# A padded DRAM copy of all edge attributes, written during the layer-0 passes of a graph network kernel

## The reference, cut to what matters

```python
# layer 0: two graph attention passes (forward over dst, backward over src), no edge attributes
x = x + gat_fwd_bwd(layernorm(x), edge_index)
x = x + experts(layernorm(x))
# layer 1
q, k, v = (z @ Wq + bq), (z @ Wk + bk), (z @ Wv + bv)     # z = layernorm(x)
e   = edge_attr @ We
k_j = k[src] + e
v_j = v[src] + e
alpha = segment_softmax(sum(q[dst] * k_j) / sqrt(32), dst)  # 8 heads of 32
out   = segment_sum(v_j * alpha, dst) + z @ Ws + bs
x = x + out
x = x + slice_attention(layernorm(x))
```

## Time and profile before

| | |
|---|---|
| Median of 3 runs | 5683.37 us (5675.45 to 5690.65) |
| Span of the profiled execution, first to last instruction | 5673.3 us |
| DVE busy | 3824.3 us (67%) |
| POOL busy | 3388.4 us (60%) |
| PE busy | 2860.0 us (50%) |
| ACT busy | 1441.9 us (25%) |
| POOL's DMA queue, share of the 16 engines' span | 28.6%, 483.60 MB |
| SP's DMA queue, share of the 16 engines' span | 24.9%, 476.59 MB |

### The profile page before, as it was taken

One profiled execution on the slowest core, in us unless ns is written; L12 is line 12 of the kernel. 1 busy time (PEld: TensorE's weight loads), 2 busy tenths in 40 slices (PEclk: granted clock), 3 DMA queues, 4 the chain that ended last, 5 costly groups with the idle time before them and its releaser, 6 DMA issues. The chain is left out here.

```text
span 5673.3 us, 49658 instructions
## 1 busy us (share of the span) xinstructions
PE 2860.0 (50%) x13052; PEld 2232.1 (39%) x13052; DVE 3824.3 (67%) x6117; ACT 1441.9 (25%) x2526; POOL 3388.4 (60%) x3382
## 2 busy tenths in 40 slices
PE   7513200000000000015899986888888888884777
PEld 5412200000000000014677633777776777673456
DVE  7357778786454545546543464989899998995763
ACT  1113333332233333311222211222222222221320
POOL 0267777777777777753440276777777777773200
PEclk9655555555555555556799998999999999896888
DMA  3133344432363333323232355999999999993114
GB/s 101 36 84 108 107 130 148 130 104 83 103 220 110 109 110 109 110 87 124 93 124 68 107 191 191 317 319 323 319 319 321 319 323 318 323 318 113 67 47 148
DMA packets 290231, 961.79 MB, mean 170 GB/s; under 512 B 79248, under 2 KB 119831, under 8 KB 248468
## 3 DMA queue, kind: packets, MB, share of 16 engines
q0 software_dynamic: 171296, 483.60, 28.6%
q1 hardware_dynamic: 118788, 476.59, 24.9%
HBM read 626.03 MB, written 345.69 MB: 171 GB/s over the span
## 5 line engine op out<-in xcount | busy, mean ns | idle before, releaser
L1249 PE MATMUL e_psE<-e_we,e_eaT 128*128 128x256 f32 x3136 | 903.5, 415 | 279.3 <-DVE e_wv L1148 179.3
L1111 POOL DMA_INDIRECT e_kv<-kv,rec x784 | 875.7, 1117 | 266.3 <-issue 253.7
L779 POOL DMA_INDIRECT g_g<-t,rec x784 | 777.1, 991 | 254.0 <-issue 253.7
L779 POOL DMA_INDIRECT g_g<-t,dst_of x784 | 743.6, 949 | 259.3 <-issue 257.2
L1249 PEld LDWEIGHTS e_psE<-e_we,e_eaT 128*128 128x128 f32 x3136 | 649.4, 210 | 400.7 <-ACT e_eaT L1192 299.4
L1407 PE MATMUL j_psM<-ident,tail 128*128 128x128 f32 x32 | 7.2, 416 | 1149.0 <-PEq L53 1149.0
L1250 PE MATMUL e_psE<-e_kv,ident 128*128 128x256 f32 x1568 | 509.8, 409 | 0.0
L816 DVE TENSOR_TENSOR_SCAN g_wv<-g_fx,g_wv 128x2176 f32<-128x2176 f32 x98 | 459.0, 4684 | 0.2 <-issue 0.2
L1407 PEld LDWEIGHTS j_psM<-ident,tail 128*128 128x128 f32 x32 | 6.8, 322 | 1149.8 <-issue 1149.8
L1118 POOL DMA_INDIRECT e_q<-q,q_of x392 | 370.9, 946 | 119.7 <-issue 119.7
L956 ACT ACTIVATE g_st<-g_wv 128x2048 f32<-128x2048 f32 x98 | 375.9, 3836 | 0.0
(11 more groups left out here) (519 smaller groups left out, 6620.8 us busy)
## 6 DMA issues: line engine op xcount, KB each, us to landing
state<-e_st SPq DMA_DIRECT2D x98, 1088.0 KB, 6.2
e_ea<-in_edge_attr SPq DMA_DIRECT2D x98, 896.0 KB, 9.8
state_f<-g_st SPq DMA_DIRECT2D x49, 1088.0 KB, 4.4
state_b<-g_st SPq DMA_DIRECT2D x49, 1088.0 KB, 4.3
m_work<-xs SPq DMA_DIRECT2D x119, 128.0 KB, 2.3
ys<-m_work SPq DMA_DIRECT2D x119, 128.0 KB, 1.7
xs<-g_ta SPq DMA_DIRECT2D x28, 512.0 KB
g_g<-t,rec POOLq DMA_INDIRECT x784
```

The lines of the kernel that those rows point to most:

```text
L779: pool.indirect_dma_start(g[:, u, j, :], None, tab, bass.IndirectOffsetOnAxis(ap=at_, axis=0)).then_inc(gat[u], 16)
L1111: pool.indirect_dma_start(kv[:, u, b, :], None, c.kv, bass.IndirectOffsetOnAxis(ap=c.rec[:, t, 1:2], axis=0)).then_inc(gkv[u][b // 4], 16)
L1249: nc.tensor.matmul(half, eaT[:, m, j, k, :], we[:, k, :], start=(k == 0), stop=False)
```

## The change

All 128 partitions' attributes are copied during the layer-0 passes, in blocks 0 to 97, one or two partitions in each block (128 partitions over 98 blocks), to a new DRAM buffer `c.ea_p`. Its rows, one for each partition, are one attribute row (1 KB) longer than they need be: neighbouring partitions lie 785 KB apart. The edge pass loads each block with one DMA for all 128 partitions from that buffer, whether the edges were sorted or not; `order_attributes` writes there if its flag is set. SP reads no flag in the edge pass and has no branch. `c.ea_sorted` and `c.ea_tail` are gone.

```diff
-            def copy_attributes(a):
+            def copy_attributes(p):
+                ea, lo = A["edge_attr_256"], p * T
+                real = min(T, E - lo)
+                spread = lambda at, n: c.ea_p[p:p + 1, at * D:(at + n) * D].rearrange("o (a n) -> (o a) n", a=16)
                 over_engines = lambda rows: rows.rearrange("(a n) w -> a (n w)", a=16)
-                ea, lo = A["edge_attr_256"], (112 + a) * T
-                real = min(T, E - lo)
-                sp.dma_start(over_engines(c.ea_tail[a * T:a * T + real, :]), over_engines(ea[lo:lo + real, :])).then_inc(other, 16)
+                sp.dma_start(spread(0, real), over_engines(ea[lo:lo + real, :])).then_inc(other, 16)
                 if real == T:
                     return 1
-                sp.dma_start(over_engines(c.ea_tail[a * T + real:(a + 1) * T, :]), over_engines(ea[0:T - real, :])).then_inc(other, 16)
+                sp.dma_start(spread(real, T - real), over_engines(ea[0:T - real, :])).then_inc(other, 16)
                 return 2
...
-                if 0 <= blk - FIRST < 16:
-                    others += copy_attributes(blk - FIRST)
+                for p in range(blk * P // NB, (blk + 1) * P // NB):
+                    others += copy_attributes(p)
...
-                        sp.dma_start(c.ea_sorted.rearrange("(p t) w -> p (t w)", p=P)[:, bass.ds((i * U + u) * (B * D), B * D)],
+                        sp.dma_start(c.ea_p[:, bass.ds((i * U + u) * (B * D), B * D)],
                                      rows[:, u, :, :]).then_inc(so[u], 16)
...
-            unsorted = c.flag_on(sp)
 
             def load_attributes(b, u):
 
-
-                at_ = bass.ds(b * (B * D), B * D)
-                rows = lambda a: a.rearrange("(p t) w -> p (t w)", t=T)[:, at_]
-                with sp.If(unsorted > 0):
-                    sp.dma_start(ea[0:112, u, :, :], rows(c.ea_sorted[0:112 * T, :])).then_inc(eg[u], 16)
-                    sp.dma_start(ea[112:P, u, :, :], rows(c.ea_sorted[112 * T:EP, :])).then_inc(eg[u], 16)
-                with sp.Else():
-                    sp.dma_start(ea[0:112, u, :, :], rows(A["edge_attr_256"][0:112 * T, :])).then_inc(eg[u], 16)
-                    sp.dma_start(ea[112:P, u, :, :], rows(c.ea_tail)).then_inc(eg[u], 16)
+                sp.dma_start(ea[:, u, :, :], c.ea_p[:, bass.ds(b * (B * D), B * D)]).then_inc(eg[u], 16)
...
-                    pe.wait_ge(eg[u], (i + 1) * 32)
+                    pe.wait_ge(eg[u], (i + 1) * 16)
...
-    c.ea_sorted = dram("ea_sorted", (EP, D))
-    c.ea_tail = dram("ea_tail", (16 * T, D))
+    c.ea_p = dram("ea_p", (P, (T + 1) * D))
```

## The result

The changed kernel takes 5688.84 us (median of 20 runs, 5678.66 to 5695.99) against 5679.49 us (20 runs, 5670.98 to 5690.65). The ratio is 1.0015, interval 1.0009 to 1.0022: 9.4 us slower. Twenty runs can tell that from nothing; it is half of the 0.3% up to which the prediction spoke of no change. The forecast was 5698 us, with "same" the likeliest sign.

The account below looks back on a forecast made before the run. DVE was taken to bound the edge pass, POOL the layer-0 passes. +11 + 2 + 4.3 - 2.5 + 0 = +14.8 us on the 5683.4 us median gave 5698 us; range of 8 in 10: 5675 to 5714 us.

Parts of the forecast that it names:

- same: Whole kernel: time within 0.3% (17 us) of the kernel before; chance 0.48, against 0.45 slower and 0.07 faster.
- DVE bounds the edge pass: Edge pass: DVE's own chain sets 16.5 us a block; saturated DMA adds at most 3 us in all.
- The faster rival: Edge pass: DMA is the bound after all, -2.3 us in each of 98 blocks, -228 us, 5470 us; chance 0.05.
- The start: Start of the edge pass: second load issue gone and the load nearer a store's speed, -2.5 us (bounds -0.4 and -4.8).
- The pitch does nothing: Edge-pass load: still lands in 10 to 11 us, start saves only 0.4 us, sum +16.9 us, 5700 us; chance 0.28.
- The pauses: Layer-0 passes: POOL's 12 stalls, one per 112 gathers; 9 get copies, 1.2 us longer each, +11 us (bounds 0 and 22).
- the sign of longer pauses: Layer-0 profile after: POOL's stalls 5 us each in the second direction if copies lengthen them, 3.9 if not.
- The last landing: Last block of the layer-0 passes: last gather lands later with a copy under way, unhidden, +2 us (bounds 0 and 2.8).
- The tail: End of the layer-0 passes: two partitions' copies behind the very last store, unhidden, +4.3 us (bounds 4 and 5).
- POOL's issue: Layer-0 passes: copies do not slow POOL's issue of gathers, booked 0 (bound above 23 us).
- The slower rival: Layer-0 passes: copies slow every gather by 13 ns, +23 us on top of the sum, 5721 us; chance 0.12.
- The sum: Whole kernel: all terms together +14.8 us, +0.26%, 5698 us; bounds -0.7 to +29.4 us, 5683 to 5713 us.

Follow-up runs that it names:

- e1_copies_only: The changed kernel's copies and buffer, with the edge pass of the kernel before (branch, two loads, PE waiting for 32): 5693.87 us, ratio 1.0026 to before.
- e4_no_padding: The changed kernel without the padding, rows of the copy 784 KB apart: 5690.21 us, ratio 1.0017 to the kernel before.
- e9_load_in_two: The changed kernel with each block's load split into two DMAs (112 and 16 partitions) from the padded buffer, no branch: 5687.46 us, ratio 1.0018 to before.

## Why the prediction was right, and where it was not

- **DVE bounds the edge pass: right.** 16.56 us a block with a tenth less DMA time in use, and 1.9 to 2.2% off the whole kernel when DVE loses one instruction. The faster rival was wrong, but by less than it looked: once DVE is lighter, the kernel with two loads is slower than the one with one, so transfers are probably what comes next behind DVE where there are two loads.
- **The start, -2.5 us: right in size (-2.0 in this pair; -3.4 from the load's issue to DVE's first instruction, the stretch that the prediction read), wrong in cause.** I put it down to a load that might run nearer to a store's speed with another pitch. It is the one DMA in place of two, at any of the three pitches. Over all runs the first gather to DVE's first product takes 25.7 to 28.6 us in the seven kernels with two loads and 20.5 to 23.7 us in the seven with one. "The pitch does nothing" was true as a mechanism; its price, +2 us on the sum, was not, since the gain did not hang on the pitch.
- **The pauses, +11 us: +10.6 us in this pair, +6.4 us in the other, by another road.** The prediction held that a late landing of a gather is hidden except in the last block. It is not before these pauses: POOL goes on only 1.77 us after DVE can first use the last gather of the block before, so that there a late landing is paid. I took each as 1.2 us longer where a copy is near, with an upper bound of 5.14 us. Three went to 6.3 to 8.0 us, beyond that bound, three stand at 5.0 to 5.1 us, and four of the second direction fell from about 3.9 to about 2.1 us, as SP's stores now came behind the gather that counts. None of the second direction is near the 5 us that the prediction named as the sign of longer pauses. That the sum came out is partly luck; the kernels that hold or move the traffic show the mechanism itself.
- **The last landing, +2 us: wrong sign, -1.7 us.** The step supposed that the copy lies ahead of the last gather; the store and copy fell after it. In e1_copies_only, e4_no_padding and e9_load_in_two, with the same copies, it is 4.4 to 4.6 us, so the term turns on a microsecond of phase.
- **The tail, +4.3 us: right, +4.5 us.** 9.77 to 9.81 us in all kernels with copies in the last block, 5.3 us in those without.
- **POOL's issue, 0: nearly right, -3 us.** The mean gather went from 991 to 989 ns and from 949 to 947 ns in the two directions; the -3 us are what the table leaves over. The slower rival's 13 ns did not come.
- **The sum, +14.8 us, measured +9.4 us.** Last landing and gathers, together some 7 us too dear, were made up in part by one wait of POOL for DVE of 1.5 us. The median of 20 runs lies well inside the range. Of the 9 us between the forecast of 5698 us and that median, 4 us come from the kernel before, whose median of 20 runs is 5679.49 us in place of the 5683.37 us of three. Added up again, the lower bounds of the terms give -0.8 us, not -0.7.

## What to carry to other kernels

A transfer that nobody waits for can still be paid for where it gets ahead of one that somebody does: look in the timeline at what lies in the queues at the moments when the bounding engine stands still, and move the extra traffic by a microsecond or two before you count its bytes. Copies for a later stage belong away from such moments and from the last block. And a share of freed DMA time is worth what the next bound allows: here nothing at 16.56 us a block, 0.25 to 0.37 us a block once DVE is lighter.

## What the runs showed of the hardware that was not expected

- POOL stands idle before the same gather, number 112k + 2 of each direction, in every kernel with gathers of 128 rows. Wherever DVE was waiting for the previous block's last gather, POOL went on 1.77 to 1.78 us after DVE's first use of it; no pause is under 1.7 us. With 64 rows a gather there are no pauses.
- Two DMAs of 112 and 16 partitions keep the DMA engines busy for a tenth more of the time than one of 128 for the same bytes at the same 321 GB/s (share 1.00 against 0.91).
- Before these pauses, the landing of a block's last gather, read where DVE waited for it, grows from 1.5 to 1.8 us with nothing ahead to between 4.6 and 6.6 us behind a store and one copy, and between 6.7 and 7.4 us behind a store and two.
